# Stacked score products, projections moved ahead and routing in another PSUM bank in a two-layer gated attention and mixture-of-experts kernel

## What is computed

```python
x = x + tanh(g_xattn[0]) * mha0(layernorm(x), ctx)        # biases, no mask
x = x + tanh(g_ffn[0])   * moe0(layernorm(x))             # 8 experts 256-1024-256, relu, softmax of the top 2 logits
x = x + tanh(g_xattn[1]) * mha1(layernorm(x), ctx, mask)  # padding and causal mask, no biases
x = x + tanh(g_ffn[1])   * moe1(layernorm(x))             # 8 experts, silu(gate) * up, width 512

# attention, per head
scores = q @ k.T / 4
out = softmax(scores - masks) @ v
```

## Time and profile before

| | us |
|---|---|
| device time, median of 3 runs | 1913.05 |
| device time, lowest and highest | 1907.3, 1914.03 |
| profiled execution, device time | 1892.92 |
| profiled execution, span from first to last instruction | 1891.1 |

### The profile page before, as it was taken

One profiled execution on the slowest core, in us unless ns is written; L12 is line 12 of the kernel. 1 busy time (PEld: TensorE's weight loads), 2 busy tenths in 40 slices (PEclk: granted clock), 3 DMA queues, 4 the chain that ended last, 5 costly groups with the idle time before them and its releaser, 6 DMA issues.

```text
span 1891.1 us, 36389 instructions
## 1 busy us (share of the span) xinstructions
PE 1672.7 (88%) x12444; PEld 1587.1 (84%) x12444; DVE 1210.5 (64%) x2859; ACT 1196.0 (63%) x2795; POOL 792.5 (42%) x877
## 2 busy tenths in 40 slices
PE   3999999998399999999975999999994599999990
PEld 2898888887399999999974998888884599999990
DVE  3465566654477777777756667767655566666655
ACT  2776566663188888888853766655562477777760
POOL 2123333323356666666652112323312366666650
PEclk9998899996599999999997999989896699999995
DMA  2112222112467777788742223322220577777758
GB/s 92 46 47 66 62 55 56 48 39 71 124 206 231 233 233 229 228 230 234 229 155 88 62 63 84 83 75 76 55 71 26 175 238 225 231 234 232 229 181 275
DMA packets 209513, 265.59 MB, mean 140 GB/s; under 512 B 28224, under 2 KB 155460, under 8 KB 209200
## 3 DMA queue, kind: packets, MB, share of 16 engines
q1 hardware_dynamic: 189840, 222.36, 40.8%
q0 software_dynamic: 13632, 35.13, 5.1%
q10 hardware_dynamic: 5856, 5.77, 1.0%
HBM read 202.89 MB, written 45.69 MB: 131 GB/s over the span
## 4 chain that ended last, share of the span: by engine, by line
PE 81%; DVE 8%; DMA 3%; issue 3%; POOL 2%; ACT 2%; SPq 1%; POOLq 0%; DVEq 0%; ACTq 0%
PE ps L363 19%; PE ps L365 19%; PE ps L364 19%; PE ps L484 10%; PE ps L383 6%; PE ps L494 2%; PE ps L465 2%; POOL xs_scr L1132 2%; PE ps L399 1%; DMA U<-ys_scr 1%; PE ps L415 1%; PE ps L458 1%; DVE X L1331 1%; DVE mx L912 1%; DMA xs_scr<-U,PI 1%
## 5 line engine op out<-in xcount | busy, mean ns | idle before, releaser
L1035 POOL TENSOR_TENSOR KXR<-U,KXR 128x1024 fp32r<-128x1024 f32 (+1 forms) x156 | 334.4, 2144 | 308.0 <-ACT KXR L645 307.2
L363 PE MATMUL ps<-QR,KXR 128*128 128x256 f32 x1248 | 355.1, 285 | 8.5 <-DVE QR L1039 8.5
L364 PE MATMUL ps<-QR,KXR 128*128 128x256 f32 x1248 | 354.7, 284 | 0.0
L365 PE MATMUL ps<-QR,KXR 128*128 128x256 f32 x1248 | 354.3, 284 | 0.0
L645 ACT ACTIVATE KXR<-U 128x1024 fp32r<-128x1024 f32 (+1 forms) x312 | 287.7, 949 | 78.0 <-PE ps L365 62.1
L555 ACT ACTIVATE U<-ps,mx 128x128 f32<-128x128 f32 x1024 | 293.9, 388 | 4.7 <-DVE mx L912 4.7
L484 PEld LDWEIGHTS ps<-VA,U 128*128 128x128 f32 x2048 | 275.8, 203 | 11.8 <-DVE U L901 1.2
L484 PE MATMUL ps<-VA,U 128*128 128x17 f32 x2048 | 264.7, 263 | 1.0 <-DVE U L901 1.0
L363 PEld LDWEIGHTS ps<-QR,KXR 128*128 128x128 f32 x1248 | 238.6, 191 | 9.7 <-DVE QR L1039 9.7
L364 PEld LDWEIGHTS ps<-QR,KXR 128*128 128x128 f32 x1248 | 238.6, 191 | 0.0
L365 PEld LDWEIGHTS ps<-QR,KXR 128*128 128x128 f32 x1248 | 238.3, 191 | 0.0
(11 more groups left out here) (190 smaller groups left out, 3949.2 us busy)
## 6 DMA issues: line engine op xcount, KB each, us to landing
U<-in_wpack SPq DMA_DIRECT2D x234, 512.0 KB, 4.1
U<-xs_scr SPq DMA_DIRECT2D x78, 257.0 KB, 4.4
U<-in_wpack SPq DMA_DIRECT2D x78, 256.0 KB, 3.6
KXR<-U SPq DMA_DIRECT2D x512, 32.0 KB, 2.0
U<-in_ctx_t SPq DMA_DIRECT2D x16, 512.0 KB, 4.1
U<-ys_scr SPq DMA_DIRECT2D x32, 256.0 KB, 3.0
U<-ys_scr SPq DMA_DIRECT2D x16, 512.0 KB, 10.2
XR<-in_L_ffn_b SPq DMA_DIRECT2D x39, 128.0 KB, 3.9
```

The costliest lines, as they stand in the source:

```text
L363: e.matmul(o, wh, xh, start=first, stop=False)
L364: e.matmul(o, wh, xl, start=False, stop=False)
L365: return e.matmul(o, wl, xh, start=False, stop=done)
L1035: e.tensor_tensor(w_cols(L, WL, n), w_raw(L, n), hi, ALU.subtract).then_inc(*l_w[n](L, i))
```

## The change

- **Scores in one product.** Q and K projections are kept as high and low parts in one buffer each (`QT`, `KT`), stored to a DRAM scratch (`qk_d`, 1 MB each per group) and loaded back so that the three parts of the contraction lie under each other: partitions 0 to 31, 32 to 63 and 64 to 95 hold q high, q low, q high of two heads (`QX`), and k high, k high, k low (`KX`), with zeros where a row belongs to the other head. One product with 96 rows and 256 columns then gives the scores of two heads; a unit has two of them, and in layer 1 two mask products of 256 columns. A half (two samples) is loaded by `sp_stack` with three DMAs for Q (256 KB each) and six for K (128 KB each), into one of two buffers.
- **Projections earlier.** The offsets are X transposes -10, -9, Q -8, -7, K -2, 0, V 4, 11, so Q of a group is made 19 to 20 steps ahead of its first scores. LayerNorm, the loads of x and of ys and the context follow; the first step is -38 instead of -21.
- **Routing in `BK`.** Transposes, logits and ranks of the routing use the bank of the projections; `uses_bk` lists all its users. DVE copies the ranks to SBUF (`RK`) one step after they are made, and the bank counts as emptied then. `BO_` is left to `ot` and `op`.
- **Routing in smaller pieces.** For all but the last group, maximum, index, selection with gates, exponential, second half of the gates, carries and row numbers stand in steps `e1` + 1, 2, 3, 4, 5, 5 and 6, the scatters from `e1 + 7`.

The same shift of offsets is made on ACT, DVE, POOL and SP; the parts of the diff that only repeat it are left out.

```diff
-        self.lt = (self.e0 + 4, self.e0 + (6 if g < NG - 1 else 5))
-        self.e1 = self.e0 + (8 if g < NG - 2 else 7 if g < NG - 1 else 6)
-        self.d = (2, 4, 5) if g < NG - 2 else (1, 3, 4) if g < NG - 1 else (1, 2, 3)
+        late = g == NG - 1
+        self.lt = (self.e0 + 4, self.e0 + 5)
+        self.e1 = self.e0 + (6 if late else 7)
+        (self.max, self.index, self.sel, self.gates, self.exp, self.gates2, self.rk, self.rank, self.rows, self.scatter) = (
+            self.e1 + k for k in ((1, 1, 1, 1, 1, 2, 2, 3, 3, 3) if late else (1, 2, 3, 3, 4, 5, 4, 5, 6, 7)))
...
-FIRST, LAST = -21, 146
+FIRST, LAST = -38, 147
+X0, Q0, K0, V0 = (-10, -9), (-8, -7), (-2, 0), (4, 11)
...
+        qk_d = [nc.dram_tensor(n, (NG, 2, 256, 1024), F32, kind="Internal").ap() for n in ("qk_scr", "qk1_scr")]
...
-        KX = KXR[:, :].rearrange("p (r z m h k) -> p r z m h k", r=2, z=2, m=2, h=8)
+        KX = KXR[:, :].rearrange("p (r c a n) -> p r c a n", r=2, c=8, a=2)
+        QX = QR[:, :].rearrange("p (r c n) -> p r c n", r=2, c=8)
...
-        KT = U1[:, 0:4096].bitcast(F32R).rearrange("p (r b z m k) -> p r b z m k", r=2, b=G, z=2, m=2)
+        KT, QT = (U1[:, i * 2048:(i + 1) * 2048].bitcast(F32R).rearrange("p (m z n) -> p z m n", z=2, m=2) for i in range(2))
...
-                    out.append((("op", b), v_xup, (0, b)))
+                for name, at, empty in (("xt", X0, v_xt), ("q", Q0, v_q), ("k", K0, v_k), ("v", V0, a_v)):
+                    for n in range(2):
+                        if (g := grp(s, at[n])) is not None:
+                            out.append(((name, g, n), empty[L, g, n]))
...
+                    if s == p.rk:
+                        out.append((("rk", p.key), v_rk[(L,) + p.key]))
...
+        def bank_free(w, *use):
+            if use in before:
+                w.wait_ge(*before[use])
...
-                    b, m, z = i // 4, (i // 2) % 2, i % 2
-                    g, j, bank = b // G, b % G, SB_[i % 3]
-                    w.wait_ge(*v_q[L, g, 1])
-                    w.wait_ge(*d_k[b % 2][L, b, 7])
+                    b = i // 4
+                    g, j, r, bank = b // G, b % G, (b // 2) % 2, SB_[i % 3]
+                    w.wait_ge(*d_k[r][L, b // 2, 5])
+                    w.wait_ge(*d_q[r][L, b // 2, 2])
                     if i >= 3:
                         w.wait_ge(*a_p[L, i - 3])
-                    js = slice(j * 128, j * 128 + 128)
-                    kh, kl = (KX[:, b % 2, p, m, 4 * z:4 * z + 4, :].rearrange("p h k -> p (h k)") for p in range(2))
-                    ins = three(e, bank[:, :], (QR[:, g % 2, 0, m, js], QR[:, g % 2, 1, m, js]), (kh, kl), True, L == 0)
                     if L == 1:
                         w.wait_ge(*v_mk[g])
                         w.wait_ge(*s_ir[0])
-                        ins = e.matmul(bank[:, :], IR[:, :], MK[:, g % 2, j:j + 1, :].to_broadcast([128, 4, 128]), start=False, stop=True)
+                    js = slice((b % 2) * 128, (b % 2) * 128 + 128)
+                    for c in range(2):
+                        o, pk = bank[:, c * 256:(c + 1) * 256].rearrange("p (a k) -> p a k", a=2), 2 * (i % 4) + c
+                        ins = e.matmul(o, QX[0:96, r, pk, js], KX[0:96, r, pk, :, js], start=True, stop=L == 0)
+                        if L == 1:
+                            ins = e.matmul(o, IR[:, :], MK[:, g % 2, j:j + 1, :].to_broadcast([128, 2, 128]), start=False, stop=True)
                     ins.then_inc(*m_s(L, i))
...
-                    if (g := grp(s, 6 + t)) is not None:
+                    if (g := grp(s, X0[t])) is not None:
                         w.wait_ge(*v_ln1[L, g])
-                        w.wait_ge(*(v_xt[L, g, 0] if t else v_k[L, g, 1]))
+                        bank_free(w, L, "xt", g, t)
...
-                    if (g := grp(s, 8 + 2 * m)) is not None:
+                    if (g := grp(s, Q0[m])) is not None:
...
-                        w.wait_ge(*(v_q[L, g, 0] if m else v_xt[L, g, 1]))
+                        w.wait_ge(*v_xt[L, g, 1])
+                        bank_free(w, L, "q", g, m)
                         pe_proj(e, L, 0, XT, m).then_inc(*m_q(L, g, m))
+                for m in range(2):
+                    if (g := grp(s, K0[m])) is not None:
+                        w.wait_ge(*s_wl[L, 1])
+                        w.wait_ge(*p_ct[L, g])
+                        bank_free(w, L, "k", g, m)
+                        pe_proj(e, L, 1, CT, m).then_inc(*m_k(L, g, m))
...
-                    if (g := grp(s, 12 + 2 * h)) is not None:
...
-                        w.wait_ge(*(a_v[L, g, 0] if h else v_q[L, g, 1]))
+                        bank_free(w, L, "v", g, h)
...
-                    w.wait_ge(*before7[0, "ot", b])
+                    w.wait_ge(*(v_xup[0, b - 1] if b else s_bov[0]))
...
-                    w.wait_ge(*before7[0, "op", b])
...
+                                ins = e.matmul(BK[:, j * E:(j + 1) * E], LT[:, t, j * 128:(j + 1) * 128], rw[:, L, t, :], start=t == 0, stop=t == 1)
                         ins.then_inc(*m_lg(*k))
-                    if s == p.e1 + p.d[1]:
+                    if s == p.rk:
...
                         sv = SEL[:, p.js].rearrange("p g e -> p (g e)")
-                        e.matmul(BO_[:, 0:p.n * E], cst[:, C_UT:C_UT + 128], sv, start=True, stop=True)
-                        e.matmul(BO_[:, 32:32 + p.n * E], cst[:, C_ONE:C_ONE + 128], sv, start=True, stop=True).then_inc(*m_rk(*k))
+                        e.matmul(BK[:, 0:p.n * E], cst[:, C_UT:C_UT + 128], sv, start=True, stop=True)
+                        e.matmul(BK[:, 32:32 + p.n * E], cst[:, C_ONE:C_ONE + 128], sv, start=True, stop=True).then_inc(*m_rk(*k))
...
+                if (g := grp(s, -4)) is not None:
...
+                        if g:
+                            w.wait_ge(*d_qd[L, g - 1])
...
+                if s == p.rk:
+                    k = (L,) + p.key
+                    w.wait_ge(*m_rk[k])
+                    w.wait_ge(*v_c.now)
+                    e.tensor_copy(RK[:, :, 0:p.n], BK[:, 0:64].rearrange("p (z g e) -> p z g e", z=2, g=G)[:, :, 0:p.n]).then_inc(*v_rk(*k))
...
-            w.wait_ge(*m_rk[k])
-            for j in range(n):
+            w.wait_ge(*v_rk[k])
+            for j in range(p.n):
                 b = p.bs.start + j
                 w.wait_ge(*v_c.now)
-                e.tensor_tensor(CR[:, b + 1], CR[:, b], BO_[:, 32 + j * E:32 + (j + 1) * E], ALU.add).then_inc(*v_c.up())
-            w.wait_ge(*v_c.now)
-            e.tensor_tensor(PX[:, js], BO_[:, 0:n * E].rearrange("p (g e) -> p g e", g=n), CR[:, p.bs], ALU.add).then_inc(*v_c.up())
+                e.tensor_tensor(CR[:, b + 1], CR[:, b], RK[:, 1, j], ALU.add).then_inc(*v_c.up())
...
-                        if (g := grp(s, -3 + j)) is not None:
...
-                    if (g := grp(s, -2 + j)) is not None:
...
-                if (g := grp(s, 2)) is not None:
+                if (g := grp(s, -14)) is not None:
...
-                if (g := grp(s, 5)) is not None:
+                if (g := grp(s, -11)) is not None:
...
+                if L == 1 and (g := grp(s, 6)) is not None:
...
-                    if s == p.e1 + p.d[0]:
-                        dve_route(e, w, L, p)
+                    if s == p.max:
+                        dve_max(e, w, L, p)
+                    if s == p.index:
+                        dve_index(e, w, L, p)
+                    if s == p.sel:
+                        dve_sel(e, w, L, p)
+                    if s == p.gates:
                         dve_gates(e, w, L, p)
-                    if s == p.e1 + p.d[1]:
+                    if s == p.gates2:
                         dve_gates2(e, w, L, p)
-                    if s == p.e1 + p.d[2]:
-                        dve_rank2(e, w, L, p)
+                    if s == p.rank:
+                        dve_rank(e, w, L, p)
+                    if s == p.rows:
+                        dve_rows(e, w, L, p)
...
+                if (g := grp(s, -4)) is not None:
...
+                if (g := grp(s, -14)) is not None and g:
...
-                        if s == p.e1 + p.d[2] + n // 2:
+                        if s == p.scatter + n // 2:
...
+        def sp_stack(e, w, L, h):
+
+            g, r, ns = h // 2, h % 2, slice((h % 2) * 256, (h % 2) * 256 + 256)
+            if h >= 2:
+                w.wait_ge(*m_s[L, 8 * (h - 2) + 7])
+            w.wait_ge(*d_qd[L, g])
+            for n in range(3):
+                src = qk_d[L][g, 0].rearrange("(c a) (z n) -> a z c n", c=8, z=2)[:, (0, 1, 0)[n], :, ns]
+                e.dma_start(QX[32 * n:32 * n + 32, r].bitcast(F32), src).then_inc(*d_q[r](L, h, n))
+            w.wait_ge(*d_kd[L, g])
+            w.wait_ge(*s_kz[L, r])
+            for n in range(6):
+                q, a = n // 2, n % 2
+                src = qk_d[L][g, 1].rearrange("(c b a) (z n) -> b a z c n", c=8, b=2, z=2)[a, :, (0, 0, 1)[q], :, ns]
```

(26 more changed lines are left out.)

189 lines of the change are left out of this document (82 added, 107 removed).

## The result

| | us | ratio to before, 95% interval |
|---|---|---|
| before, median | 1911.7 (1907.3 to 1914.0) | 1 |
| changed, median | 1994.7 (1984.0 to 2005.4) | 1.044 [1.038, 1.050] |
| changed, profiled execution | 1984.0 device time, span 1981.7 | |

The forecast was 1855, range 1785 to 1908. The change makes the kernel 83 us slower. The two profiled executions differ by 91 us, and the windows of both, cut at the same events, say where. "Low clock" is TensorE's time at 1.2 GHz in the stretch, summed from the granted clock; 2 x (1 - PEclk) x length gives it too, within 4 us for the attentions. In the profiled execution of before the mean granted clock is 0.920, in its timed runs beside the experiments 0.900 to 0.916, so its 67 and 44 us of low clock are less than it usually has.

A forecast was written before the change was run, and what follows sets the result against it. TensorE was taken to bound both attentions, 788 of 1891 us. Terms -118 - 62 - 13 + 65 + 66 + 4 = -58 us, subtracted from the timed median of 1913.05, gave 1855 us, range 1785 to 1908.

The forecast's parts named there:

- Part 1: Attention scores: two 256-column products with 96 rows replace three of 512, saving 0.46 us a step, 118 us.
- on PE, which ends the steps: Both attentions: TensorE sets the step length, so the 118 us of saved score work counts in full.
- Part 2: Routing in the projections' bank, spread over steps: 62 us of waits and low clock gone, 65 us of new ones added.
- the old waits: Attentions: TensorE waiting for PI (2.26 us) and layer 1's exponential (1.93 us), said to start most low-clock stretches and to go.
- inside the 2 us: Attentions: ys loads late behind stack waits on SP, counted within the 2 us a group put on waits.
- Part 3: Projections many steps ahead: starts longer by 30 and 36 us in the two layers, 13 us less in the steps.
- Part 4: Score stack through DRAM: transfers hidden under the steps, price 0; without cover, 8 us a half.
- Part 5: Last routing after each attention: ranks, row numbers and scatters start later, +2 us a layer, +4 in all.
- TensorE stays at its lower clock: Rival, chance 0.12: layer 0's steps between projections run at low clock, 1.3 us more each; 1965 us in all.
- Other engines take over: Rival, chance 0.15: VectorE's bursts keep attention groups near 46 and 44 us; 1898 us, about no change.
- The pipeline swallows the waits: Rival, chance 0.18: attention waits fit under other work and low-clock stretches vanish with the stalls; 1785 us.
- the stacked product isn't cheaper: Rival, chance 0.03: the new score products save nothing, so the 118 us is not there; 1973 us.

The follow-up runs named there:

- e3: The kernel before with two of its three score products left out and nothing else changed: ratio 0.980 to before.
- e12_rk: The kernel before with ranks copied out of bank 7, freeing it earlier, and the gates' exponentials one step later: 1889.5 us, ratio 0.978.
- e14: e12_rk with two of its three score products left out: 1831.3 us, ratio 0.959 to the kernel before.
- e13: The changed kernel with reordered starts, three row buffers, routing back in bank 7 at its old steps, rank copy and later exponentials: ratio 1.002 to before.
- e9_route: The kernel before with routing in the projections' bank, spread over more steps, and K, V and half of Q in the new steps: ratio 1.012.
- e10_traffic: The kernel before with 64 MB of unread DRAM-to-DRAM copies added behind each sample's K copies: ratio 1.003.
- experiments 3 and 6: Two of three score products left out, on the kernel before (0.980) and on e12_rk (0.959, against 0.978 without the cut).
- experiment 4: The changed kernel with q/k stores and stack loads of group 0 only: 1.013, 60 us less; also extra DRAM copies on the kernel before: 1.003.
- experiment 1: The changed kernel with its scatters one step earlier: 1948.8 us, ratio 1.017 to the kernel before.

## Why the prediction was wrong

PE's time in the two attentions can be split in three. The first is its busy time, with the part of it at the lower clock counted half: the work, as it would be at the full clock. The second is the other half of that part: the cost of the low clock. The third is its idle time. From the profiled executions, in us, rounded:

| kernel | work | cost of low clock | idle | sum |
|---|---|---|---|---|
| before | 735 | 55 | 31 | 821 |
| changed | 619 | 157 | 65 | 840 |
| before, one of three products (e3) | 623 | 130 | 42 | 794 |
| e12_rk | 741 | 40 | 36 | 818 |
| e12_rk, one of three products (e14) | 623 | 102 | 35 | 760 |
| stack with that routing (e13) | 624 | 132 | 34 | 790 |

That the work comes out at 731 to 741 us in the four profiled kernels with three products (e9_route and e10_traffic too), with 82 to 190 us of low clock, is what supports counting half. Three-pass products of 512 columns stand 0.23 us apart at the full clock and 0.43 at the lower one.

**Part 1 (-118).** The term was right in size, 0.44 us a step by the bare steps of layer 1 at the full clock, and wrong in worth: the step that failed is "on PE, which ends the steps", which priced the saved work at a clock of 1. Cutting the same work alone gave 38 and 37 us (experiments 3 and 6), and by the table the lower clock took back 75 of 113 us there and 62 of 118. In the changed kernel it took 102 us of 116. In layer 0 the AV bank took 0.3 us of most bare steps.

**Part 2 (-62 + 65).** Two small edits against the old waits gave 41 of the 62 us. Between e12_rk and e9_route (0.978 to 1.012) lie 64 us, against 65, but that is partly luck: they came with 82 us more of low clock, 9 us more idle time and steps of K, V and Q that were not varied by themselves. The low clock was put at 2 us a group, 32 in all. The one-bank waits of Q were seen, the wait for the scatters was not. The step of the scatters is in the diff, one later, and the prediction moved it past no queue: GpSimd's Newton steps stood in the way, and 50 us hung on it. The prediction put everything else that is late "inside the 2 us", which gave it no price.

**Part 3 (+66, -13).** The starts cost 64. The absolute bounds 1055 to 1065 for layer 1's first score failed (1082.9) only because the 25.6 us of layer 0 came before it; from the last expert product it is +33. The 13 us given back in the steps were not separated by any run.

**Part 4 (0).** Wrong by some 60 us (experiment 4), and with the wrong question. Stack loads did land in time; VectorE's and GpSimd's other transfers did not, and the bound of 8 us a half priced only the stack's own lateness.

**Part 5 (+4).** +8.

**What was missing in sum**: 147 us in the two attentions. By the table the work fell by 116 us where 131 (118 and 13) were counted, 15 us missing; small gaps that the profile counts as busy are in it, like those in layer 0's bare steps. The cost of the low clock, 342 us of it for 111, rose by 102 where the sum had it nearly even (32 in, 39 of the 62 out), some 109. PE's idle time rose by 34 where some 9 were counted (32 in, the old waits of 23 out), 25. Removing the traffic takes away parts of these, so its 60 us don't add to them.

**The rivals.** *TensorE stays at its lower clock* had the mechanism, at 0.12. Its price of a bare step, 1.3 us, measured 1.54 (in layer 1, with the mask). Its place was too narrow: it looked at layer 0 between projections, and the clock fell in both layers, about half of the times at the logit products, the longest stretches among them. Its "against" failed: dense Q, K, V stretches did not always bring the clock back; stretches lasted up to 47.8 us where the example in the earlier trace rows had 6.8. The Trainium skill ("TensorE: Matmul & The Clock Gate", A second HAM failure mode) ties such falls to short idle times between bursts; the windows of experiment 1 show a fall without any in the last 6.6 us. *Other engines take over* is part of it: ScalarE waits 31 us for VectorE's maxima in attention 1. *The pipeline swallows the waits* is refuted, and so is *the stacked product isn't cheaper*: products stand 0.12 us apart.

The range ended at 1908, 87 us short. The prediction's own bounds went further: 130 for part 2 alone gives 1920, the low-clock rival 1965, and 8 us a half for part 4 would be 256 us over 32 halves. The range took in none of the three, and two of them came together: low clock and late transfers.
